# Attention pipeline of a two-layer kernel: GpSimd's order around the output norm, and the norm and the row gates two steps later

## The reference

```python
h = _layernorm(x) * (1 + ca) + sa
x = x + ga * _L0_attn_ref(h, ...)        # a recurrence with decays, 512 steps
h = _layernorm(x) * (1 + cb) + sb
x = x + gb * _L0_ffn_ref(h, weight, bias)  # one 128x128 product, operands rounded to 6 bits
h = _layernorm(x) * (1 + ca) + sa
x = x + ga * _L1_attn_ref(h, ...)
h = _layernorm(x) * (1 + cb) + sb
x = x + gb * _L1_ffn_ref(h, ...)
```

```python
out = g[:, 0] * a1 + g[:, 1] * a2 + g[:, 2] * a3
return out.transpose(0, 2, 1, 3).reshape(B, T, 512) @ w_proj
```

```python
ft = sigmoid(xt @ wf.T + c @ uf.T + bf)
it = sigmoid(xt @ wi.T + c @ ui.T + bi)
gt = tanh(xt @ wc.T + c @ uc.T + bc)
c = ft * c + it * gt
```

## Time and profile before

| | |
|---|---|
| median of 3 runs | 1850.0 us (1849.26 to 1852.9) |
| profiled execution, its own time | 1854.49 us |
| its span | 1852.7 us |
| mean granted clock of TensorE | 0.961 of full |
| PE busy | 1715.3 us, 93% |
| ACT busy | 1220.4 us, 66% |
| DVE busy | 1158.5 us, 63% |
| POOL busy | 680.2 us, 37% |

### The profile page before, as it was taken

One profiled execution on the slowest core, in us unless ns is written; L12 is line 12 of the kernel. 1 busy time (PEld: TensorE's weight loads), 2 busy tenths in 40 slices (PEclk: granted clock), 3 DMA queues, 4 the chain that ended last, 5 costly groups with the idle time before them and its releaser, 6 DMA issues.

```text
span 1852.7 us, 33815 instructions
## 1 busy us (share of the span) xinstructions
PE 1715.3 (93%) x10588; PEld 1067.9 (58%) x10588; DVE 1158.5 (63%) x3679; ACT 1220.4 (66%) x3383; POOL 680.2 (37%) x697
## 2 busy tenths in 40 slices
PE   5676689999999999999999999999999999999998
PEld 3433456665566656665666566665666566656664
DVE  5999666656555656655665656565565566565675
ACT  2564367766776757776676677675777677667773
POOL 0456533444333333434344433333333434443300
PEclk8787799999999999999999999999999999999999
DMA  4001021112111211212111211121122211121101
GB/s 171 1 0 28 17 64 41 41 37 64 27 43 36 51 44 41 52 45 52 41 41 36 64 29 43 38 50 42 41 52 45 52 41 41 40 62 30 42 19 46
DMA packets 71295, 80.91 MB, mean 44 GB/s; under 512 B 29520, under 2 KB 37840, under 8 KB 70992
## 3 DMA queue, kind: packets, MB, share of 16 engines
q1 hardware_dynamic: 71120, 78.76, 17.2%
HBM read 7.91 MB, written 2.10 MB: 5 GB/s over the span
## 4 chain that ended last, share of the span: by engine, by line
PE 72%; DVE 9%; ACT 8%; issue 6%; POOL 4%; DMA 0%; SPq 0%; DVEq 0%; POOLq 0%; ACTq 0%
PE bank L1862 24%; PE bank L1883 13%; PE bank L1826 8%; PE bank L1716 4%; PE bank L1717 3%; ACT arena L1002 2%; PE bank L1774 2%; PE bank L1789 2%; PE bank L1836 2%; DVE arena L1452 1%; PE bank L1712 1%; PE bank L1780 1%; PE bank L1783 1%; PE bank L1671 1%; PE bank L1770 1%
## 5 line engine op out<-in xcount | busy, mean ns | idle before, releaser
L1002 ACT ACTIVATE arena<-arena 128x512 f32<-128x512 f32 (+3 forms) x1024 | 571.4, 559 | 314.0 <-DVE arena L1452 309.2
L1452 DVE CUSTOM_DVE_ANT_0 arena<-bank,W 128x512 f32<-128x512 f32 (+3 forms) x1024 | 478.6, 487 | 464.9 <-PE bank L1862 436.7
L1862 PE MATMUL bank<-arena 96*128 96x512 f32 (+3 forms) x2048 | 698.8, 443 | 0.0
L1862 PEld LDWEIGHTS bank<-arena 96*128 96x128 f32 x2048 | 351.1, 192 | 192.6 <-issue 127.4
L1883 PE MATMUL bank<-W,arena 128*128 128x128 f32 x2560 | 420.1, 278 | 9.1 <-ACT arena L1002 7.1
L1883 PEld LDWEIGHTS bank<-W,arena 128*128 128x128 f32 x2560 | 309.6, 142 | 175.5 <-issue 103.7
L994 ACT ACTIVATE arena<-bank 128x512 f32<-128x512 f32 (+1 forms) x512 | 277.4, 542 | 126.4 <-PE bank L1883 121.6
L739 POOL TENSOR_TENSOR arena<-arena,one 128x512 f32<-128x512 f32 x64 | 66.5, 1040 | 722.3 <-DVE arena L1420 558.5
L1002 ACT ACTIVATION_READ_ACCUMULATOR arena<-arena 128x1 f32 x1024 | 195.9, 191 | 0.0
L1463 DVE COPY arena<-bank 128x384 f32<-128x384 f32 x256 | 141.8, 554 | 63.8 <-PE bank L1883 63.8
L1826 PE MATMUL bank<-arena 128*32 128x256 f32 (+1 forms) x3072 | 166.7, 350 | 0.0
(11 more groups left out here) (255 smaller groups left out, 2079.8 us busy)
## 6 DMA issues: line engine op xcount, KB each, us to landing
arena<-arena SPq DMA_DIRECT2D x896, 64.0 KB, 2.0
arena<-arena SPq DMA_DIRECT2D x64, 128.0 KB, 2.4
W<-wide SPq DMA_DIRECT2D x1, 3730.0 KB, 13.3
X<-x SPq DMA_DIRECT2D x8, 256.0 KB, 5.8
out<-arena SPq DMA_DIRECT2D x8, 256.0 KB, 2.3
arena<-arena SPq DMA_DIRECT2D x96, 16.0 KB, 1.8
LW<-lat SPq DMA_DIRECT2D x1, 768.5 KB, 14.3
arena<-mods SPq DMA_DIRECT2D x1, 768.0 KB, 4.7
```

Source lines behind the costliest of these rows:

```text
L1002: done = A(here, here, ACT.Exp, bias=nmax[:, c:c + 1], scale=-1.0, accum_out=lsum[:, c:c + 1])
L1452: last = v.tensor_tensor_reduce(Pb[:, s % 4, at_p:at_p + n], bank[turn.score_bank(s)][:, at:at + n], w("mask", T - n), -1.0, 3e38, ALU.add ...
L1862: last = MM(B_[:, at:at + n], query(t), Kb[a][g % 2][0:QD, h, 0:n], start=True, stop=True)
```

## The change

Three edits. In GpSimd's list of a full turn `repeat(turn, 6)` stands in front of `norm_out(i)` and not behind it. `normed_out` moves from unit 11 to unit 13 of the g = 0 group, on DVE. In the table for g = 0 (not in the first group) z4T moves from unit 13 to 15, gf from 15 to 17 and gi from 16 to 18; gc stays at 19. No instruction is added or removed. The parts `FIRST` and `LAST` are not touched, so that all of it happens 7 times.

```diff
@@ group_tasks
-        extra = [...] if first else [(13, "z4T"), (15, "gf"), (16, "gi"), (19, "gc")]
+        extra = [...] if first else [(15, "z4T"), (17, "gf"), (18, "gi"), (19, "gc")]
@@ gpsimd, a full turn
                 rope(turn, "q", 4)
                 rope(turn, "k", 4)
+                repeat(turn, 6)
                 norm_out(i)
-                repeat(turn, 6)
 
                 pool.wait_ge(s_g, turn.filled("op", NG - 2))
                 gate_proj(i + 1)
@@ vector, attend
-                        if at == 11:
+                        if at == 13:
                             normed_out(turn.b)
```

More of the change, by code:

```diff
@@ L83, in group_tasks @@
         steps, proj = {"op": 7, "s2": 9, "o2": 20}, (0, 1, 3, 6, 8, 5, 11, 21, 22)
-        extra = [(7, "z3T"), (11, "score"), (12, "vs"), (13, "gates"), (21, "rank")] if first else [(13, "z4T"), (15, "gf"), (16, "gi"), (19, "gc")]
+        extra = [(7, "z3T"), (11, "score"), (12, "vs"), (13, "gates"), (21, "rank")] if first else [(15, "z4T"), (17, "gf"), (18, "gi"), (19, "gc")]
     if first:
```

## The result

The changed kernel takes 1839.24 us in the median of 6 runs (1836.84 to 1839.87), the kernel before 1849.49 (1847.68 to 1852.9) in the runs that go with them. The ratio is 0.9936, with a 95% interval of 0.992 to 0.9953. A second set of runs of the same two kernels gave 1838.79 against 1849.63 and 0.994 (0.9919 to 0.9962). One run of the kernel before in that set, 3185.07 us at a granted clock of 0.852, is left out of the ratio. The quotient of the two medians of the first set is 0.9945, inside its interval but not equal to its ratio. So the change makes the kernel 0.6% faster: 10 us by the medians, 12 by the ratio, 9 to 15 by its interval. The forecast was 1832 us and a gain of 18. The profiled execution has a span of 1835.9 us, against 1852.7 before, and a mean granted clock of 0.967, against 0.961.

The account below looks back on a forecast made before the run. PE, busy 93% of the span, bounds the kernel, and one late chain costs it two waits. 2.40 - 0.42 = 1.98 us a turn, seven times 13.9, plus 4 for the clock, off 1850.0: forecast 1832 us, range 1826 to 1841.

Parts of the forecast that it names:

- Step 1: PE's waits at z4T and the spread: the old waits go, gain 2.40 us a turn, bounds 2.14 and 2.76.
- Step 2: GpSimd's norm_out behind repeat: deviation ready 0.1 us before DVE reaches normed_out, cost 0.
- The margin of 0.1 us: At unit 13: norm_out ends at 1801.80, DVE reaches normed_out at 1801.91 on the last group's clock.
- Step 3: normed_out at unit 13: rows ready 2.6 us behind the spread, PE at z4T 2.96; no wait, by 0.4 us.
- The stretch: normed_out slowed beside GpSimd's gate_proj, lengthening the wait at gf: 0.36 us, seven times, 2.5 us less gain, 1834.6 us.
- Step 4: Gates at units 17 to 19: PE waits 0.42 us at gf for ACT's read of z4T, bounds 0 and 0.92.
- Step 5: Clock drops behind the two old waits in three turns: all 6.3 us go; 4 us taken off the median.
- the drop at 662 to 666 us: Behind the edited spread in one turn: clock at 0.59 of full, that turn's interval 29.50 us against 26.95.
- Rival 1: Clock drops move to other turns or places: 1836.1 us, 1839 with half as many new drops; 17%.
- rival 4: Unit 13: DVE waits for norm_out, repeat late by 1 us; gain 1.0 a turn, 1839 us; 11% with The stretch.
- Rivals 2 and 3: Gates: rival 2 hands the gain back, 1849 us, 7%; rival 3 adds clock drops in all turns, 1863 us, 5%.

Follow-up runs that it names:

- e1: Changed kernel with the deviation (norm_out) put back ahead of the repeat of the inverses: 1842.16 us, ratio 0.9925; run again 1838.87 us, 0.9933.
- e2: Changed kernel with GpSimd's gate products L725 moved behind the repeat of the next row: 1834.84 us, ratio 0.9905.
- e6: Changed kernel with vw at unit 13 instead of 21, deviation ahead of the repeat, gate products behind the next repeat: 1827.68 us, ratio 0.9878.
- e7: Changed kernel with the table's edit undone (z4T at 13, gf 15, gi 16), normed rows still at unit 13: 1875.33 us, ratio 1.013.
- e3: Changed kernel with deviation ahead of the repeat and gate products behind the next repeat: 1838.78 us, ratio 0.9917.

## Why the prediction was right, and by how much too large

**Right: which waits go, and that it is faster.** The direct wait at z4T and the indirect one at the spread were one late chain, and both went with the move. The range and the sign held; the gain was 10 us by the medians where 18 were forecast.

**Step 1, the old waits.** 2.40 us a turn were forecast from the last group of LAST. The way to the edited spread fell from 26.93 to 24.19 us, 2.74, of which 0.47 is z4T's place: 2.27 us. The stand-in was good to 0.13 us, its remaining idle 0.36 us came as 0.41.

**Step 2, norm_out behind repeat: cost 0.** Wrong by a little, and for a reason of its own: 1.39 us was read from a stretch in which DVE stood idle. Behind repeat, L744 falls beside L1385 and takes 0.65, not 0.20 us, and norm_out ends 0.31 us later than forecast. The margin of 0.1 us turned into DVE's wait of 0.24. Experiment e1 shows that with the old order the repeat starts no later, so with the other two edits in place this one had nothing to give and cost 0.56 us a turn.

**Step 3, normed_out at unit 13: "no wait, by 0.4 us".** This is the step that failed. DVE starts 0.24 us late and the four instructions take 1.53 us for 1.11, 0.66 us together. The margin was not 0.4 us to begin with: PE starts z4T 0.15 us behind the end of L1351, before the change (458.37 to 458.52) and after it (461.90 to 462.05), and the sum left this out. So z4T starts 3.36 us behind the spread and not 2.96, and PE waits 0.35. The stretch stood in the prediction as a case beside the sum, at 0.36 us a turn and 2.5 us in all. By e2 it costs 0.43 us a turn, 3.0 us in all. That the sizes are close is luck: the 0.36 us was the spread of the durations of L1385, another instruction, and was put on the wait at gf, while it shows at z4T. I had put it outside the sum since no row of before showed L1351 beside GpSimd. The Trainium skill ("GPSIMD Engine Reference", section "Key points") says that DVE instructions in a two-port mode or with two SBUF inputs contend with GpSimd. The trace agrees for the second kind: GpSimd's L744 loses 0.45 us beside DVE's L1385, which has two SBUF inputs. DVE's L1351 has one SBUF tensor input and loses 0.10 us an instruction beside L725, as e2 shows; no run here shows which mode it is in.

**Step 4, the first gate.** 0.42 us forecast, 0.49 found, and by the mechanism of the forecast: DVE's late maximum keeps ACT back, and ACT's read of z4T is late by it. In all profiles with z4T at 15 L966 starts 2.81 us behind the end of L1351, and the gate starts when it ends. So an earlier end of the rows moves the gate too. The wait stays at 0.49 us in e1 and e2, where PE comes to the gate earlier by the same amount, and is gone in e6, where the rows end 1.1 us earlier behind the spread than in the changed kernel. The whole way behind the edited spread grew by 28.43 - 26.95 - 0.47 = 1.01 us a turn; its waits are 0.35 + 0.49, and 0.17 have no wait of their own in the profile. Matmuls that follow without a wait overlap, and a wait ends that overlap: from L1883 to L1655 take 0.90 us with the wait of 0.35, and 0.38 in e6 without one. The sum had nothing for this.

Together 2.27 - 1.01 = 1.26 us a turn, 8.8 us, for the 13.9 of the sum.

**Step 5, the clock.** That the drops behind the edit go was right: none in seven turns, 6.3 us less in the profile. But in the plain runs the gain is 10.3 to 10.8 us as a difference of medians, so beyond the 8.8 us there is room for 1.5 to 2 us, where I took 4. The ratio's interval, 9 to 15 us of gain, leaves 0 to 6 us, so this size isn't settled. That the profiled execution of before, 4.5 us above its median, had more of these drops than the usual run would explain the difference; only one execution of before has a trace, so it isn't shown. The prediction also called the drop at 662 to 666 us the work of a long idle gap. The gaps there were of 1.46 and 1.04 us, and the same two left the clock up in four of the seven turns; the 4.64 us of e7 brought it down in all seven. Rival 1 (no gain from the clock, 1836.1 us) and rival 4 (the thin margin at unit 13 fails, 1839 us) each hold a part of what came. Rival 4 has the mechanism, with GpSimd's contention in place of a late repeat. Its time is right by luck: it counts 7 us of waits and 4 of clock, where 8.8 and about 2 came. Rivals 2 and 3, waits at the next gates, did not occur: gi and gc show none.

**Open.** The span fell by 16.8 us between the two profiles, the medians by 10. 15.1 of the 16.8 are around the edit. What moves the clock at the keys isn't settled, since no kernel here edits that group. Among the kernels with the normed rows at unit 13, the five profiles with the deviation ahead of the repeat lost 10.3 to 12.2 us there and the six with it behind, e7's included, 5.7 to 8.2. But the kernel before has the deviation ahead as well and lost 6.7, so the order alone does not do it. It could be the point of the turn at which the keys' group falls; no kernel here moved that alone. Nor does the loss at the keys alone explain why the times of e1 and e3 don't follow their waits: the part ahead of the loop, from 261.6 to 267.3 us in these profiles, moves the span as much, and it differs by 3.7 us between two executions of the same kernel.

## What to carry to other kernels

When a step is moved to where its input will just be ready, take the duration of the instructions that make the input from a place where the same neighbour engine is at the same work: here a GpSimd instruction of 0.20 us took 0.65 and a margin of 0.1 us was none. The trace of before had the sign: in each turn the L725 that started beside the same DVE instruction took 0.86 us and the others 0.41. And add the time from the end of one engine's work to the start of the other's, 0.15 us here. A late chain is cured at its user, with other ready work put into the hole; vw at unit 13 gave 8 us beside the 10 of the change itself. And judge an edit of one place by the intervals around it as well as by the run: 4 us of waits less can vanish when the clock elsewhere and the part ahead of the loop vary by as much as 6 us each.

## What the runs showed of the hardware that was not expected

- A GpSimd instruction on 128x4 numbers takes 0.20 us alone and 0.65 us when it starts beside DVE's L1385 (two SBUF inputs, 128x512); with the deviation ahead of the repeat it is 0.20 again, and then the first L725, of 128x128, takes 0.86 for 0.41 us beside L1385. DVE's L1351 (128x128, one SBUF tensor input) takes 0.342 us alone and 0.445 beside GpSimd's L725.
- What the clock takes at the keys has a pattern within one execution and another in the next of the same kernel: the second profile of the changed kernel has 27.42 to 27.62 us there in all seven turns, the first 29.07 and then 26.53 and 28.2 by turns, at spans of 1836.9 and 1835.9 us.
